# Attention and spiking feed-forward kernel: projection directly behind the scores, block transposition last on VectorE, reciprocal sums and output transposed in one PSUM bank

## The reference, cut to what matters

```
xn  = layernorm(x)                       # outer norm, no scale or bias
h   = layernorm(xn) * ln_scale + ln_bias
c_q, c_kv = h @ w_down_q.T, h @ w_down_kv.T        # 64 latents each
q, k, v   = c_q @ w_up_q.T, c_kv @ w_up_k.T, c_kv @ w_up_v.T   # 16 heads
q, k      = rope(q), rope(k)                       # pairs (even, odd) rotated
attn      = softmax(q k^T / 8)
a         = (attn @ v) @ w_out.T + xn
y         = relu(xn @ W_fc.T)**2 @ W_proj.T        # 512 hidden
spikes    = 5 steps of a leaky integrator fed with y, counted, / 5
out       = x + a + spikes
```

## Time and profile before

| | before |
|---|---|
| runs | 1335.43, 1337.35, 1348.48 us (median 1337.35) |
| profiled execution | 1334.07 us, its span 1332.3 us |
| PE busy | 1093.0 us (82%) |
| PEld busy | 753.1 us (57%) |
| DVE busy | 984.1 us (74%) |
| ACT busy | 837.0 us (63%) |
| POOL busy | 804.2 us (60%) |
| TensorE clock granted, mean | 0.96 |
| HBM traffic | 9 GB/s |
| all DMA traffic | 164 GB/s, mostly inside the core's own memory |

### The profile page before, as it was taken

How to read it: one execution, slowest core, us unless ns; L and a number is a source line. 1 busy time by engine, 2 the same in 40 slices (tenths; PEclk the granted TensorE clock), 3 DMA queues, 4 the chain that set the end, 5 groups by cost and what they waited for, 6 DMA issues and landing times.

```text
span 1332.3 us, 25712 instructions
## 1 busy us (share of the span) xinstructions
PE 1093.0 (82%) x6880; PEld 753.1 (57%) x6880; DVE 984.1 (74%) x1350; ACT 837.0 (63%) x2945; POOL 804.2 (60%) x837
## 2 busy tenths in 40 slices
PE   3678888889788888788888888888888888788886
PEld 2446555556555655556555555555556656556654
DVE  3677788777787777777777787677778777777772
ACT  2666666666666666665666665566666666666650
POOL 3567556566656557656667656566566566656550
PEclk9899999989999999999999999999999999999998
DMA  4466676676576565675665675665676666676562
GB/s 147 118 181 157 158 190 171 165 177 162 157 185 164 161 175 153 166 180 145 179 175 157 167 185 155 162 178 143 167 191 160 171 177 163 160 181 170 160 166 62
DMA packets 93273, 217.87 MB, mean 164 GB/s; under 512 B 22464, under 2 KB 43200, under 8 KB 93120
## 3 DMA queue, kind: packets, MB, share of 16 engines
q1 hardware_dynamic: 72768, 150.45, 48.8%
q10 hardware_dynamic: 20480, 67.13, 13.4%
HBM read 7.77 MB, written 4.19 MB: 9 GB/s over the span
## 4 chain that ended last, share of the span: by engine, by line
PE 32%; issue 28%; POOL 20%; DVE 12%; ACT 4%; SPq 1%; DVEq 1%; DMA 1%; POOLq 0%; ACTq 0%
PE ps_s L300 12%; PE ps_u L318 9%; POOL partner L740 6%; POOL qk L743 6%; PE ps_b L396 5%; DVE neg_max L605 4%; POOL relu_sb L780 4%; PE ps_a L369 4%; DVE turned L614 3%; ACT prob L482 3%; POOL rstd L755 2%; DVE u_n L628 1%; DVE qk L600 1%; PE ps_qk L291 1%; PE ps_qk L290 1%
## 5 line engine op out<-in xcount | busy, mean ns | idle before, releaser
L482 ACT ACTIVATE prob<-ps_s,neg_max 128x256 f32<-128x256 f32 x1024 | 472.0, 476 | 392.8 <-DVE neg_max L605 356.5
L740 POOL TENSOR_TENSOR partner<-partner,rope_sb 128x512 f32<-128x512 f32 x256 | 325.7, 1272 | 437.5 <-DMA partner<-raw 437.3
L605 DVE TENSOR_REDUCE neg_max<-ps_s 128x4 f32<-128x1024 f32 x256 | 312.5, 1221 | 216.9 <-PE ps_s L300 216.6
L318 PE MATMUL ps_u<-gathered,ckv 128*64 128x256 f32 x2048 | 288.4, 403 | 88.9 <-ACT rden_t L553 60.3
L300 PE MATMUL ps_s<-qk 64*128 64x256 f32 x2048 | 307.5, 421 | 45.7 <-POOL qk L743 45.7
L743 POOL TENSOR_TENSOR qk<-qk,partner 128x512 f32<-128x512 f32 x256 | 325.4, 1271 | 20.1
L614 DVE STREAM_TRANSPOSE turned<-prob 128x1024 f32<-128x1024 f32 x256 | 314.4, 1228 | 1.3 <-ACT prob L482 0.4
L300 PEld LDWEIGHTS ps_s<-qk 64*128 64x128 f32 x2048 | 185.1, 195 | 162.8 <-issue 78.1
L318 PEld LDWEIGHTS ps_u<-gathered,ckv 128*64 128x64 f32 x2048 | 133.3, 140 | 164.4 <-issue 105.4
L482 ACT ACTIVATION_READ_ACCUMULATOR prob<-ps_s,neg_max 128x1 f32 x1024 | 212.1, 207 | 0.0
L600 DVE TENSOR_TENSOR qk<-ps_qk,rope_sb 128x512 f32<-128x512 f32 x256 | 171.2, 669 | 49.3 <-PE ps_qk L291 48.4
(11 more groups left out here) (57 smaller groups left out, 887.0 us busy)
## 6 DMA issues: line engine op xcount, KB each, us to landing
gathered<-turned SPq DMA_DIRECT2D x1024, 128.0 KB, 2.4
partner<-raw ACTq DMA_DIRECT2D x256, 256.0 KB, 2.5
x_sb<-in_x SPq DMA_DIRECT2D x32, 128.0 KB, 2.4
resid<-xn_sb SPq DMA_DIRECT2D x32, 128.0 KB, 2.0
out<-out_sb SPq DMA_DIRECT2D x32, 128.0 KB, 1.8
turned<-in_wup SPq DMA_DIRECT2D x2, 512.0 KB, 6.1
rope_sb<-in_rope SPq DMA_DIRECT2D x1, 512.0 KB, 7.1
turned<-in_wo_t SPq DMA_DIRECT2D x1, 512.0 KB, 8.4
```

What stands on the lines that cost most here:

```text
L318: last = nc.tensor.matmul(ps_u[h * L:(h + 1) * L, 0, :], ckv[:, (s // PAIRS) % 2, kt, :], gathered[:, (s // GROUP) % 2, :, s % GROUP, h, k ...
L482: last = nc.scalar.activation(prob[:, s % 2, :, h, :, t, :].rearrange("p j k c -> p k j c"), ps_s[:, s % 2, h, t, :].rearrange("p (k j c) ...
L605: nc.vector.tensor_reduce(neg_max[:, s % 2, :, :], ps_s[:, s % 2, :, :, :], AXIS_X, ALU.max, negate=True).then_inc(max_ready, 1)
L740: nc.gpsimd.tensor_tensor(other, other, sin_sb, ALU.mult).then_inc(sin_ready, 1)
```

## The change

The output products' bank is `ps_b`. The transposed sum now goes to its first half and the transposed reciprocals to its second; `ps_u` holds the weighed latents alone, and the two waits quoted above are gone. In their place `copy_rden` waits for `final_done` and `finish` waits for the transposition of the reciprocals (`rt_ready`), because both touch `ps_b`.

On PE, `project` moves from behind `extras` to directly behind `scores`. All four chunks of `broadcast_rden` run at p0 to p3 of the following sequence; `attention_out` runs at p4, p5 and twice at p6; `transpose_rden` moves from p6 to p7, behind `transpose_sum`. On ACT, `copy_projected` and `exchange` move directly behind `exponentials`, ahead of the relu and of all work that occurs once per sequence, and `copy_rden` becomes the first instruction of p0 of the next sequence. On DVE the order becomes `row_max`, `rotate`, `normalise_u` (p0 to p3), then one of `moments_of` (p0), `split_latents` (p3), `invert_sums` (p4, before at p1), `finish` (p7), and behind these `turn`; `integrate` stays last. On POOL, `inverse_std` moves from p1 to p0 behind the rotation, the two squares from p0 and p1 to p1 and p2, `split_sums` from p2 to p5. The number of compute instructions stays the same.

The diff, without the hunks that only give `ps_u` another shape:

```diff
--- before.py
+++ after.py
@@ -307,16 +307,12 @@
                 if s % GROUP == 0:
                     pe.wait_ge(moved[(s // GROUP) % 2], (i * (BODY // GROUP // 2) + s // GROUP // 2 + 1) * 16 * Q * Q)
                 pe.wait_ge(u_evac, done(g - 1))
-                if s % PAIRS == 6:
-                    pe.wait_ge(rt_evac, done(i * UNROLL + s // PAIRS))
-                elif s % PAIRS == 7 and not outside(i * UNROLL + s // PAIRS - 1, B):
-                    pe.wait_ge(final_done, done(i * UNROLL + s // PAIRS - 1))
                 if s % PAIRS == 0:
                     pe.wait_ge(ckv_ready, done(i * UNROLL + s // PAIRS))
                 for kt in range(TT):
                     for h in range(2):
                         last = nc.tensor.matmul(
-                            ps_u[h * L:(h + 1) * L, 0, :], ckv[:, (s // PAIRS) % 2, kt, :],
+                            ps_u[h * L:(h + 1) * L, 0:S], ckv[:, (s // PAIRS) % 2, kt, :],
                             gathered[:, (s // GROUP) % 2, :, s % GROUP, h, kt, :, :].rearrange("p i t r -> p t i r"),
                             start=(kt == 0), stop=(kt == TT - 1))
                 last.then_inc(u_ready, 1)
@@ -373,16 +369,14 @@
 
             def transpose_rden(b):
                 pe.wait_ge(rden_split, done(b))
-                pe.wait_ge(u_evac, done(PAIRS * b + 5))
+                pe.wait_ge(acc_ready, done(b - 1))
                 for t in range(TT):
-                    last = nc.tensor.transpose(ps_u[:, 1, t * P:(t + 1) * P], rden_hl[:, t, :].bitcast(F32), ident_sb[:, :])
+                    last = nc.tensor.transpose(ps_b[:, S + t * P:S + (t + 1) * P], rden_hl[:, t, :].bitcast(F32), ident_sb[:, :])
                 last.then_inc(rt_ready, 1)
 
             def broadcast_rden(b, c):
                 pe.wait_ge(rt_evac, done(b))
-                if c == 0:
-                    pe.wait_ge(acc_ready, done(b - 1))
-                else:
+                if c > 0:
                     pe.wait_ge(u_norm, done(CHUNKS * b + c - 1))
                 for j in range(2):
                     last = nc.tensor.matmul(ps_b[:, j * S:(j + 1) * S], sel_sb[:, 2 * c + j, :], rden_t[:, :],
@@ -399,12 +393,8 @@
 
             def transpose_sum(b):
                 pe.wait_ge(acc_ready, done(b))
-                if not outside(b + 1, B):
-                    pe.wait_ge(u_evac, done(PAIRS * (b + 1) + PAIRS - 2))
-                else:
-                    pe.wait_ge(u_evac, done(STEPS - 1))
                 for t in range(TT):
-                    last = nc.tensor.transpose(ps_u[:, 0, t * D:(t + 1) * D], acc_t[:, t * P:(t + 1) * P], ident_sb[:, :])
+                    last = nc.tensor.transpose(ps_b[:, t * D:(t + 1) * D], acc_t[:, t * P:(t + 1) * P], ident_sb[:, :])
                 last.then_inc(fin_ready, 1)
 
             def value_by_output():
@@ -414,22 +404,25 @@
                         pair = half * PAIRS // 2 + j
                         for h in range(2):
                             rows = slice(h * DH, (h + 1) * DH)
-                            last = nc.tensor.matmul((ps_u[:, :, :].rearrange("p j s -> p (j s)"), ps_b)[half][h * L:(h + 1) * L, j * D:(j + 1) * D],
+                            last = nc.tensor.matmul((ps_u, ps_b)[half][h * L:(h + 1) * L, j * D:(j + 1) * D],
                                                     wv_sb[rows, pair, :], wo_sb[rows, pair, :],
                                                     start=True, stop=True)
                 last.then_inc(setup_pe, 1)
 
             def extras(b, b0, p):
                 if not outside(b - 1, B):
-                    if p < 3:
-                        broadcast_rden(b - 1, p + 1)
-                    elif p < 7:
-                        attention_out(b - 1, p - 3)
+                    if p < 4:
+                        broadcast_rden(b - 1, p)
+                    elif p < 6:
+                        attention_out(b - 1, p - 4)
+                    elif p == 6:
+                        attention_out(b - 1, 2)
+                        attention_out(b - 1, 3)
+                    elif p == 7:
+                        transpose_sum(b - 1)
                 if p == 7:
                     if not outside(b, B):
-                        broadcast_rden(b, 0)
-                    if not outside(b - 1, B):
-                        transpose_sum(b - 1)
+                        transpose_rden(b)
                     if not outside(b + 1, B):
                         ffn_in(b + 1, 0, 1 - b0)
                 if not outside(b, B):
@@ -437,8 +430,6 @@
                         ffn_in(b, 1, b0)
                     elif p in (4, 5):
                         ffn_out(b, p - 4)
-                    elif p == 6:
-                        transpose_rden(b)
                 if p == 1 and not outside(b + 1, B):
                     latents_by_token(b + 1)
                 if not outside(b + 2, B):
@@ -460,9 +451,9 @@
                 b = i * UNROLL + b0
                 if not outside(g + LEAD["scores"], STEPS):
                     scores(g + LEAD["scores"], s + LEAD["scores"])
-                extras(b, b0, p)
                 if not outside(g + LEAD["project"], STEPS):
                     project(g + LEAD["project"], s + LEAD["project"], i)
+                extras(b, b0, p)
                 if not outside(g, STEPS):
                     weigh_latents(g, s, i)
 
...
@@ -548,9 +539,10 @@
 
             def copy_rden(b):
                 act.wait_ge(rt_ready, done(b))
+                act.wait_ge(final_done, done(b - 1))
                 if not outside(b - 1, B):
                     act.wait_ge(bc_ready, done(CHUNKS * (b - 1) + CHUNKS - 1))
-                nc.scalar.copy(rden_t[:, :], ps_u[:, 1, :]).then_inc(rt_evac, 1)
+                nc.scalar.copy(rden_t[:, :], ps_b[:, S:2 * S]).then_inc(rt_evac, 1)
 
             def prologue():
                 start_counters(act, "act")
@@ -562,13 +554,16 @@
             def step(i, s):
                 g, b0, p = i * BODY + s, s // PAIRS, s % PAIRS
                 b = i * UNROLL + b0
+                if p == 0 and not outside(b - 1, B):
+                    copy_rden(b - 1)
                 if not outside(g + LEAD["scores"], STEPS):
                     exponentials(g + LEAD["scores"], s + LEAD["scores"], i)
-                if not outside(b, B):
-                    if p == 0:
-                        relu(b, 1)
-                    elif p == 6:
-                        copy_rden(b)
+                if not outside(g + LEAD["project"], STEPS):
+                    copy_projected(g + LEAD["project"], s + LEAD["project"], i)
+                if (s + LEAD["project"]) % 2 == 1 and not outside(g + LEAD["project"], STEPS):
+                    exchange(g + LEAD["project"], s + LEAD["project"])
+                if p == 0 and not outside(b, B):
+                    relu(b, 1)
                 if not outside(b + 1, B):
                     if p == 1:
                         copy_latents(b + 1, 1 - b0)
@@ -582,12 +577,8 @@
                         copy_inputs(b + 2, b0)
                     elif p == 3:
                         lead_latents(b + 2, b0)
-                if not outside(g + LEAD["project"], STEPS):
-                    copy_projected(g + LEAD["project"], s + LEAD["project"], i)
                 if not outside(g, STEPS):
                     copy_u(g, s, i)
-                if (s + LEAD["project"]) % 2 == 1 and not outside(g + LEAD["project"], STEPS):
-                    exchange(g + LEAD["project"], s + LEAD["project"])
 
             run(act, prologue, step)
 
@@ -668,10 +659,12 @@
 
             def finish(b, par, i):
                 dve.wait_ge(fin_ready, done(b))
+                if not outside(b + 1, B):
+                    dve.wait_ge(rt_ready, done(b + 1))
                 dve.wait_ge(copied[par], 16 * (i + 1))
                 dve.sem_inc(dve_waited, 1)
                 dve.wait_ge(stored[par], 16 * (i + 1))
-                nc.vector.tensor_tensor(out_sb[:, par, :, :].rearrange("p t d -> p (t d)"), ps_u[:, 0, :],
+                nc.vector.tensor_tensor(out_sb[:, par, :, :].rearrange("p t d -> p (t d)"), ps_b[:, 0:TT * D],
                                         resid[:, par, :], ALU.add).then_inc(final_done, 1)
 
             def prologue():
...
@@ -701,23 +694,22 @@
                     add_spikes(b - 1, 1 - b0)
                 if not outside(g + LEAD["scores"], STEPS):
                     row_max(g + LEAD["scores"], s + LEAD["scores"])
-                if p == 1 and not outside(b, B):
+                if not outside(g + LEAD["project"], STEPS):
+                    rotate(g + LEAD["project"], s + LEAD["project"])
+                if p < 4 and not outside(b - 1, B):
+                    normalise_u(b - 1, p)
+                if p == 0 and not outside(b + 2, B):
+                    moments_of(b + 2, b0, i + 1)
+                elif p == 3 and not outside(b + 2, B):
+                    split_latents(b + 2, b0)
+                elif p == 4 and not outside(b, B):
```

(32 more changed lines are left out.)

5 lines of the change are left out of this document (2 added, 3 removed).

## The result

| | before | after |
|---|---|---|
| median of the runs | 1338.58 us (4 runs) | 1376.55 us (4 runs, 1372.12 to 1379.85) |
| ratio to before | 1 | 1.0269, 95% interval 1.0204 to 1.0333 |
| span of the profiled execution | 1332.3 us | 1370.3 us |
| mean granted clock | 0.96 | 0.951 |

The change makes the kernel 2.7% slower. The forecast was 1400 us, range 1328 to 1440; the direction, the mechanism and the range held, the time was forecast 23 us too large.

What follows compares the result with a forecast made beforehand. No engine is full; waits passing between engines set the pace. Walked period 40.5 us plus 1.1 slow clock gives 41.6 against 39.54; +64 us over 31 periods on 1334.1 makes 1398, so 1400 us, range 1328 to 1440.

Steps and rivals of the forecast that it cites:

- The new waits: PE waits of 3.2 us before p4's projection, 2.2 before p2's input transpositions, 1.8 before p0's first broadcast.
- The issue on ACT: Issuing an exchange's two DMAs holds ACT 1.4 us, now ahead of the small jobs of p1, p3 and p7.
- Rival 1: The exchange costs ACT little where it now stands, so three terms of 1.4 us vanish: 1268 us; chance 0.10.
- rival 2: Waits for ACT and DVE are slack another order takes up; only removed waits count: 1215 us; chance 0.05.
- The walk at full clock: One period followed across engines from p0's first broadcast to the next: 40.5 us at 2.4 GHz.
- The first leg: p0 to p1 on DVE: from the first broadcast to the row maxima of p1, 3.3 us.
- The period of before: Mean period of the kernel before, 39.54 us, from 31 intervals of an instruction occurring once per sequence.
- The sum: Walked period plus slow clock, 41.6 us against 39.54: +2.1 us per period, +64 us over 31.
- The slow clock of the change: One stretch at 1.2 GHz in every period, because PE's idle times become longer: 1.1 us per period.
- `turn` behind the split: On DVE the 1.19 us `turn` follows `split_latents`, so p4's row maxima start at 21.0; p5's projection waits 0.4 us.
- The added waits: `finish` waiting for `rt_ready` and `copy_rden` for `final_done`, sharing one bank: 0, at most 0.4 us per period.
- ramp and tail: Start and end of the run execute the same instructions: taken as nothing, between -5 and +5 us.

Runs made afterwards that it cites:

- e9: Changed kernel plus unused matmuls inside two PE waits, 20 in p4 before the projection and 13 in p2 before the input transpositions; 1341.0 us, ratio 1.0027 to before.
- e1: Changed kernel with the exchange issued last in ACT's step, behind the small jobs and the copy of the latent product; 1260.52 us, ratio 0.9443 to before.
- e6: Kernel before with only the new order of projection, projected copy, exchange, rotation and block transposition; banks, broadcasts and reciprocals as before; 1443.22 us, ratio 1.083.
- e4: Changed kernel with projection, projected copy, exchange and block transposition back at their old places, keeping the new bank and steps; 1289.63 us, ratio 0.964 to before.
- e8: Changed kernel with the exchange issued last in ACT's step in p3 only; 1374.2 us, ratio 1.0295 to before.
- e2: Changed kernel with the block transposition ahead of the split of the latents in p3; 1376.63 us, ratio 1.0296 to before.
- e3: Changed kernel with the projection of p4 alone back behind the output and feed-forward products; 1377.01 us, ratio 1.0308 to before.
- e5: Changed kernel with 20 unused matmuls on PE in p4, ahead of the wait for the split latents; 1374.99 us, ratio 1.0307 to before.
- e10: Kernel of e7 with the projection of p4 alone behind the output and feed-forward products; 1202.28 us, ratio 0.9022 to before.
- e7: Kernel of e1 with p7's exchange behind the copy of the reciprocals and p3's block transposition before the split; 1249.49 us, ratio 0.9355 to before.

## Why the prediction was right

Time from the first broadcast, which is 723.68 in the timeline of the changed kernel above; beside it the same places in e9, which has the order of the changed kernel, its two longest waits filled and the full clock:

| step | predicted, full clock | changed kernel | e9 |
|---|---|---|---|
| row maxima of p1 | 3.3 | 727.18: 3.5 | 3.5 |
| input transpositions | 10.4 | 734.11: 10.4 | 10.3 |
| row maxima of p3 | 13.0 | 736.86: 13.2 | 13.1 |
| projection of p4 | 19.9 | 743.49: 19.8 | 19.6 |
| row maxima of p4 | 21.0 | 744.67: 21.0 | 20.9 |
| projection of p5 | 24.7 | 708.48 + 41.06: 25.9 | 24.6 |
| row maxima of p7 | 34.1 | 717.54 + 41.06: 34.9 | 33.7 |
| next broadcast | 40.5 | 40.9 to 41.1 | 39.8 |

- **The new waits** were right in place, and two of three in size: 3.2, 2.2 and 1.8 predicted, 3.26, 2.15 and 1.23 measured; in totals 100, 70 and 56 predicted, 98.5, 65.9 and 38.8 measured. The third was a third too large.
- **The issue on ACT** was right as a mechanism: 1.4 us per exchange predicted, 1.2 to 1.3 measured (37.0 to 39.9 us over 31 times). Rival 1, that it costs little, is refuted by e1. (It is argued there with seven steps of eight; an exchange stands in the odd steps only, so it is three of four.) That the whole new order costs and the bank part pays is shown by e6 and e4; rival 2 counted only the second. That within the order it is the place of the exchange that costs is shown by e1 beside e4; the prediction also counted the moved projection and the moved `turn` against it, and with the exchange last these do no net harm.
- **The walk at full clock was 0.6 us too long**, 40.5 for the 39.9 of e9. The first leg was 0.2 too short; the excess lies in three others, here as the changed kernel has them: p3 to p4 took 6.6 us for 6.9 predicted, mostly because the issue holds ACT for 1.8 to 1.9 us from the projected copy and not for 1.96; p5 to p7 9.1 for 9.4; p7 to the next broadcast 6.1 for 6.4. In p5 the pace of PE was exactly right (708.48 to 712.95, 4.47 us): the projection takes 0.57 for 0.75 and the output products 0.86 for 0.97, but the feed-forward products 0.96 for 0.68. The 0.3 us were gained in p6, where there are eight output products and no feed-forward products.
- **The period of before was taken too low.** The sum starts from 39.54 us, which has the tail in it; 39.81 is right (above). From the same number it follows that the slow clock cost before 0.5 us per period. It was more: the eight inner periods of before without a slow stretch take 38.4 to 39.7 us, mean 38.9, so it cost 0.9.
- **The slow clock of the change** was predicted at one stretch per period and 1.1 us. The trace has one in every steady period, at 40.95 - 39.9 = 1.1 us, and by the medians e9 gives 1376.55 - 1341.0 = 35.6 us, 1.15 per period. This was luck in good part. The size was taken from the middle of the periods before, and the reason given, that PE's idle times become longer, does not hold as a rule: e8 shortened the longest wait and has some 228 us at the slow clock instead of 134, and e4 has a wait of 2.2 us in every period and only 62.
- **`turn` behind the split** was on the walk with 0.4 us of margin. At the slow clock PE is later than DVE there, so it cost nothing (e2). The walk was made at full clock and missed that; in e9 the projection of p5 does wait 0.43 us for the projected copy, as the walk has it.
- **The added waits** of `finish` and `copy_rden` cost nothing to be seen, as predicted: `finish` waited for PE twice, 2.0 us in all, and `copy_rden` has no wait in the list but the issue in front of it.

Put together: predicted were +2.06 us per period, 64 us in all; measured are +1.14 and 38. The terms that were off are the walk (0.6 x 31 = 19 us too much) and the period of before (0.27 x 31 = 8 us too much), less the 3 us of ramp and tail that were taken as nothing; together that is within 2 us of the 26 by which the sum was too high.

At full clock the change costs 39.9 - 38.9 = 1.0 us per period, and this is nearly all of the 1.14. The slow clock costs 1.1 where it cost 0.9 before.

## What to carry to other kernels

A DMA issued from ACT's queue cost ACT its issue time, 1.2 us here, where too little work stood between it and the instruction that it waits for. With the copies and the four activations of p1 between the two, in e1, it cost nothing and left 0.03 us behind its data. One short instruction was not enough: in p1 of before the exchange stood last as well, with only the copy below between, and the next exponential waited 1.13 us for the issue.

```profile
714.54 0.36 ACT L510 COPY u_raw<-ps_u 128x256 f32<-128x256 f32 x1
```

Nor must the work between wait for another engine itself: in p5 of e1 the exchange left 0.27 us behind its data, because the copy of the latent product in front of it waited for PE.

When work is moved ahead "to start it earlier", look first at which instruction behind it somebody waits for. And when an edit takes a wait away without any gain, read the clock of the whole period before giving the edit up: together with the next one it may pay.

## What was not expected of the hardware

The slow stretch is not bound to one wait. In the changed kernel it came at the same place in every period, behind the wait of 3.26 us:

```profile
739.00:743.40 4.40, 1.23 (x10) 0.99 0.51 165
743.40:747.00 3.60, 3.51 (x11) 0.54 0.00 0
```

Shorten or fill that wait, and it appeared behind the wait of 2.15 us instead (e3, e5), or behind both (e8), with the same total time within 3 us in all three. In the profiled executions of e1 and e10, whose longest waits in nearly all steady periods are 1.4 and 1.7 us, and in e9 with both long waits filled, it nearly vanished; in the other runs of e1 it did so less (clock 0.961 to 0.971). So three edits that each shortened or filled a wait by 1 us or more left the time as it was, and others gave more than they removed. The length of the longest wait does not decide it alone: e4 has 2.2 us in front of the first broadcast in every period and the full clock in more than half of them, while in e7 slow stretches follow waits of 1.2 us. Why before, with waits of up to 2.0 us, had it in some periods and not in others stays open; no run was made on it.
